# Order of the score products, the weights' transposes and three copies in a windowed-attention stack, and of one copy in a causal attention

## The reference, cut to what matters

```python
mod = (silu(c) @ wmod).reshape(8, 6, 1, 128)         # sa, ca, ga, sb, cb, gb
h = layernorm(x) * (1 + ca) + sa                     # x: 8 x 512 x 128
x = x + ga * attention(h)                            # causal, 16 heads of 8 channels
h = layernorm(x) * (1 + cb) + sb
for i in range(6):                                   # 16 heads of 64 channels
    t = shift_tokens(h)
    q, k, v = split(t @ Wqkv[i])                     # 512 x 1024 each
    q, k = rotary(l2norm(q) * qs, l2norm(k) * ks)
    s = 8 * q @ k.T                                  # windows of 32, each sees itself and the one before
    h = softmax(mask(s)) @ v @ Wo[i] + h
    t = shift_tokens(h); a, g = split(layernorm(t) @ W1[i] + b1[i])
    h = (a * gelu(g)) @ W2[i] + b2[i] + h
x = x + gb * h
```

## Time and profile before

| what | value |
|---|---|
| median of three executions | 4340.35 us |
| the profiled execution, its own time | 4333.15 us |
| its span in the profile | 4331.4 us |
| granted TensorE clock over the span | 0.98 of full speed |
| first attention / stack / last part, about | 0 to 780 / 780 to 4306 / 4306 to 4331 us |

### The profile page before, as it was taken

One profiled execution on the slowest core, in us unless ns is written; L12 is line 12 of the kernel. 1 busy time (PEld: TensorE's weight loads), 2 busy tenths in 40 slices (PEclk: granted clock), 3 DMA queues, 4 the chain that ended last, 5 costly groups with the idle time before them and its releaser, 6 DMA issues. The chain is left out here.

```text
span 4331.4 us, 109584 instructions
## 1 busy us (share of the span) xinstructions
PE 3791.1 (88%) x42284; PEld 2925.6 (68%) x42284; DVE 3346.0 (77%) x4472; ACT 2494.9 (58%) x3301; POOL 2742.1 (63%) x2200
## 2 busy tenths in 40 slices
PE   5888887499998999998999989999899998999996
PEld 3555555377777777777777767777677776777774
DVE  3555555488888888888888878888888888788884
ACT  2555555266665666665666656666566665566663
POOL 2444442276766676766676767676767677767772
PEclk9999999699999999999999999999999999999998
DMA  1111110222223222222222222222322223222221
GB/s 39 46 63 67 68 61 13 65 67 58 56 57 90 66 56 57 59 77 71 62 60 54 66 85 63 55 64 53 87 65 64 56 57 87 64 62 56 57 56 59
DMA packets 157178, 267.01 MB, mean 62 GB/s; under 512 B 32062, under 2 KB 51644, under 8 KB 152380
## 3 DMA queue, kind: packets, MB, share of 16 engines
q1 hardware_dynamic: 157116, 266.19, 22.9%
HBM read 44.81 MB, written 26.21 MB: 16 GB/s over the span
## 5 line engine op out<-in xcount | busy, mean ns | idle before, releaser
L817 POOL TENSOR_TENSOR st_qk_rot<-st_qk_rot,st_qk_sq 128x1024 f32<-128x1024 f32 x384 | 920.6, 2398 | 919.1 <-DVE st_qk_sq L714 919.1
L457 PE MATMUL st_ps<-st_wqkv,st_xs 128*128 128x512 f32 x3456 | 957.8, 413 | 76.2 <-DMA st_wqkv<-wqkv_parts 38.1
L565 ACT ACTIVATE st_qk_sq<-st_ps 128x1024 f32<-128x1024 f32 x384 | 394.0, 1026 | 662.3 <-PE st_ps L457 661.7
L457 PEld LDWEIGHTS st_ps<-st_wqkv,st_xs 128*128 128x128 f32 x3456 | 613.1, 191 | 240.4 <-issue 134.6
L837 POOL TENSOR_TENSOR st_qk_rot<-st_qk_rot,st_rn 128x1024 f32<-128x1024 f32 x384 | 723.1, 1904 | 15.1
L696 DVE TENSOR_REDUCE st_nt<-st_qk_sq 128x16 f32<-128x1024 f32 x384 | 465.6, 1212 | 184.8 <-ACT st_qk_sq L565 184.7
L714 DVE TENSOR_TENSOR st_qk_sq<-st_ps,st_rot 128x512 f32<-128x512 f32 x768 | 490.2, 678 | 0.0
L700 DVE TENSOR_TENSOR st_qk_rot<-st_ps,st_rot 128x1024 f32<-128x1024 f32 x384 | 465.9, 1213 | 7.8 <-PE st_ps L472 7.8
L1444 DVE TENSOR_REDUCE at_nmx<-at_s 128x1 f32<-128x512 f32 (+3 forms) x512 | 238.1, 487 | 296.4 <-PE at_s L1094 295.6
L472 PE MATMUL st_ps<-consts_sb,st_qk_rot 128*128 128x128 f32 x3072 | 402.3, 274 | 27.8 <-DVE st_hid L797 16.7
L465 PEld LDWEIGHTS st_ps<-st_oT,st_wo 128*128 128x128 f32 x3072 | 368.8, 192 | 79.4 <-issue 74.9
(11 more groups left out here) (141 smaller groups left out, 6732.8 us busy)
## 6 DMA issues: line engine op xcount, KB each, us to landing
st_v_bd<-st_v_tok SPq DMA_DIRECT2D x1152, 128.0 KB, 2.4
st_v_bd<-st_v_tok SPq DMA_DIRECT2D x672, 64.0 KB, 2.1
wqkv_parts<-at_w_parts SPq DMA_DIRECT2D x18, 1024.0 KB, 4.6
st_wqkv<-wqkv_parts SPq DMA_DIRECT2D x18, 1024.0 KB, 5.5
at_w_raw<-in_wqkv SPq DMA_DIRECT2D x18, 512.0 KB, 5.2
rotary_tables<-at_rot SPq DMA_DIRECT2D x6, 512.0 KB, 3.3
st_rot<-rotary_tables SPq DMA_DIRECT2D x24, 128.0 KB, 2.4
st_wo<-in_wo SPq DMA_DIRECT2D x6, 512.0 KB, 4.4
```

Of the source, the lines that this page charges most:

```text
L457: last = pe.matmul(out[:, c * 512:(c + 1) * 512], xs[:, x_part, t * P:(t + 1) * P], rhs, start=(n == 0), stop=(n == len(PASSES) - 1))
L565: act.activation(qk_sq[:, cols_of(a)], slot_of("qk"[a], 0, t), ACT.Square).then_inc(squared[a], 1)
L817: pool.tensor_tensor(qk_rot[:, cols], qk_rot[:, cols], qk_sq[:, cols], ALU.add).then_inc(rot_done[a], 1)
```

## The change

In the stack: (1) on PE sim goes ahead of pt; sim takes banks 6 and 7 and pt takes banks 2 and 3, the pair of the other; the single-bank jobs m1, m2 and y move from bank 7 to bank 1 and z from bank 6 to bank 0. (2) On ACT the copy of v goes ahead of the exponential. (3) On ACT the two instructions of the reciprocal norm go ahead of the copy of pt. (4) On DVE the softmax sum and its reciprocal go from behind L772 to right behind the maximum L739, ahead of L745, L749, L756, L764 and L772. In the first attention: (5) on ACT `pick_shifted` goes from the end of the step to right behind the exponential of unit 1, ahead of that of unit 2.

```diff
-            feed = {3: [(("m1", -1, 0), (7,))], 0: [(("m2", -2, 0), (7,))], 1: [], 2: [(("y", -2, 0), (7,))]}[t]
+            feed = {3: [(("m1", -1, 0), (1,))], 0: [(("m2", -2, 0), (1,))], 1: [], 2: [(("y", -2, 0), (1,))]}[t]
             hidden = [(("h", -2, j), H_BANKS[j]) for j in range(HC)] if t == 1 else []
             return [tile("q", 0, 0, 1), tile("tq", 1, 2, 3), tile("k", 0, 4, 5), tile("tk", 1, 6, 7),
-                    tile("v", 0, 2, 3), tile("ot", 3, 0, 1), tile("pt", 2, 6, 7), tile("sim", 1, 2, 3), *feed,
-                    tile("z", 3, 6), tile("o", 2, 4, 5), *hidden]
+                    tile("v", 0, 2, 3), tile("ot", 3, 0, 1), tile("sim", 1, 6, 7), tile("pt", 2, 2, 3), *feed,
+                    tile("z", 3, 0), tile("o", 2, 4, 5), *hidden]
...
@@ scalar, stack
-                        if alive(u, d2):
-                            act.wait_ge(shifted, n - 2)
-                            act.activation(s[:, t2 % 2, :], s[:, t2 % 2, :], ACT.Exp).then_inc(exp_ready, 1)
                         if alive(u, 0):
...
                             act.activation(v_tok[:, par, :], slot_of("v", 0, t), ACT.Copy).then_inc(taken["v"], 1)
+                        if alive(u, d2):
+                            act.wait_ge(shifted, n - 2)
+                            act.activation(s[:, t2 % 2, :], s[:, t2 % 2, :], ACT.Exp).then_inc(exp_ready, 1)
...
+                        if alive(u, 0):
+                            reciprocal_norm()
                         if alive(u, d2):
...
                             act.activation(probT[:, :], slot_of("pt", d2, t2), ACT.Copy).then_inc(taken["pt"], 1)
-                        if alive(u, 0):
-                            reciprocal_norm()
@@ vector, stack
                             dve.tensor_reduce(mx[:, par, :], scores, AX.X, ALU.max).then_inc(max_ready, 1)
+                        if alive(u, d2):
+                            dve.wait_ge(exp_ready, n - 2)
+                            dve.tensor_reduce(den[:, t2 % 2, 0, :], ...).then_inc(den_ready, 1)
+                            dve.wait_ge(den_ready, 2 * (n - 2) - 1)
+                            dve.reciprocal(den[:, t2 % 2, 1, :], den[:, t2 % 2, 0, :]).then_inc(den_ready, 1)
...
                             last.then_inc(taken["z"], 1)
-                        if alive(u, d2):
...
@@ scalar, first attention
                                 if h % GROUP == GROUP - 1 and alive(b, d):
                                     max_parts(b, d, h // GROUP)
+                            if u == 1:
+                                d, h = head_of(s, LAG - 1)
+                                if alive(b, d):
+                                    pick_shifted(b, d, h)
...
-                        d, h = head_of(s, LAG - 1)
-                        if alive(b, d):
-                            pick_shifted(b, d, h)
```

More of the change, by code:

```diff
@@ L739, in unit @@
                             dve.tensor_reduce(mx[:, par, :], scores, AX.X, ALU.max).then_inc(max_ready, 1)
+                        if alive(u, d2):
+                            dve.wait_ge(exp_ready, n - 2)
+                            dve.tensor_reduce(den[:, t2 % 2, 0, :], s[:, t2 % 2, :].rearrange("p (h k) -> p h k", h=HEADS),
+                                              AX.X, ALU.add).then_inc(den_ready, 1)
+                            dve.wait_ge(den_ready, 2 * (n - 2) - 1)
+                            dve.reciprocal(den[:, t2 % 2, 1, :], den[:, t2 % 2, 0, :]).then_inc(den_ready, 1)
                         if t == 3 and alive(u, -1):
```

## The result

The changed kernel took 4167.38 us (median of 4 executions, 4166.82 to 4174.56) against 4340.39 us (4337.48 to 4353.66) of the kernel before on the same chip: a ratio of 0.9599, with a 95% interval of 0.9577 to 0.9622. It is 4% faster; the forecast was 4178 us.

The account below looks back on a forecast made before the run. PE was taken as the bound, waiting for ACT's exponential in the stack and the copy of q in the attention. 4333.15 - 82 (stack) - 80 (attention) = 4171, plus 7.2 for the median: 4178 us; 8-in-10 range 4145 to 4280.

Parts of the forecast that it names:

- attention: First attention: the copy of q falls into ACT's idle time, gaining 80 of PE's 85.3 us wait; bounds 40 and 92.
- tile t = 3: Stack, 15.81 us from q to q: 0.7 us gained, with DVE's chain, not PE, setting the next q.
- tile t = 0: Stack, 15.97 us: DVE's chain ends 15.7 us after q, next q near 15.85; gain 0.1 us.
- tile t = 1: Stack, 20.92 us: L684 is served earlier, h starts near 15.55 us after q against 15.76; gain 0.2 us.
- tile t = 2: Stack, 18.27 us: DVE is done before PE, so the gap and the restart are gained, 0.7 us.
- The gap ahead of pt: Stack: PE's wait for ACT's exponential, 0.59 us in each of 147 tiles, goes when sim runs first.
- my own sign of being wrong: Stack: the prediction fails if PE stands over 0.3 us ahead of q in t = 3 or t = 2.
- Hidden at no cost: Stack: the earlier reciprocal norm and earlier copy of v on ACT delay nothing; cost zero.
- The copy of q brought all, not half: Rival, first attention: norm chains get late behind the moved copy, gain only 40 us, 4218 us; chance 0.10.
- The stack's gap didn't only move: Rival, stack: PE waits for q's banks instead of the exponential in every tile, no gain, 4260 us; chance 0.06.
- L684 didn't stay behind L865: Rival, tile t = 1: L684 stays late, tile costs 1.9 us more, stack 19 us slower, 4279 us; chance 0.06.
- POOL doesn't keep the port: Rival, tile t = 1: POOL's back-to-back instructions block L764, h starts 6.6 us late, 4505 us; chance 0.06.

Follow-up runs that it names:

- the third experiment: The changed kernel with the softmax sum and its reciprocal put back behind the add of z on DVE: 4103.2 us, ratio 0.9442.

## Why the prediction was right

The total came out 11 us under the forecast, 4167 for 4178. The mechanism held, but that the total is so near is in part luck: the stack gave 11 us less than forecast, the attention 15.5 more, and the 7 us added for the distance of the median from the profiled execution were not there in the changed kernel (0.4).

| term | forecast | measured |
|---|---|---|
| tile t = 3 | 0.7 gained (15.1) | 0.50 (15.31) |
| tile t = 0 | 0.1 (15.85) | 0.51 (15.46) |
| tile t = 1 | 0.2 | 0.0 (20.93) |
| tile t = 2 | 0.7 (17.55) | 0.96 (17.31) |
| regular unit | 1.7 (69.3) | 1.96 (69.01) |
| whole stack | 82 us | 71 us |
| attention | 80 us | 95.5 us |

- **The gap ahead of pt** went as said: the wait is gone, the exponential ends ahead of pt's turn, L735 starts 9.93 after q in t = 3 as worked out.
- **t = 3.** DVE's chain ends 14.9 after q, forecast 15.0; but q starts 0.39 behind it, for which I took 0.14. In t = 0 that distance is 0.05. Why it is longer in t = 3 no run shows; the q behind t = 3 is also the first product of a new turn of the loop over units, which was not tried apart. The 0.40 us of PE's idle time ahead of that q also meets my own sign of being wrong (over 0.3). The sign was set too tight, since what I wrote of q, that DVE sets its start, is what happened.
- **t = 0.** L735 starts at 10.50 as said. I added up 0.74 from L749 to the z add and measured 0.54, the sum and its reciprocal took 0.1 less, and the last step 0.05, not 0.14.
- **t = 2.** PE sets this tile, as said. I counted the gap (0.57 in the tile before) and 0.1 for the restart, which no run shows by itself. From sim's start to that of y it is 2.82 (2019.65 to 2022.47) where from pt's it was 3.09 (2071.15 to 2074.24): the order itself is worth 0.27 more.
- **t = 1.** L684 was served at POOL's boundary, ahead of L865, as forecast, and this is the step on which the sign of the result hung. But the second L837 ended 2.36 after q, not 1.9: I took POOL's time from the unit before, while q itself had moved up against it. So L684 ended at 2.91, L735 started at 10.74 instead of 10.4, L771 at 14.56 instead of 14.3, and the 0.2 were lost. I also wrote that the change doesn't touch ot's wait for the first L714 pair. It did, by the same early L684: 1.4 us less in t = 1. PE got to h earlier by that and stood there for the z add, which the softmax sum holds back, so none of it was gained.
- **Hidden at no cost** was wrong for the early norm. I asked who on ACT and POOL needs it and when, and not what POOL's earlier L837 collides with. At the ends of five layers it met L771. With the regular gain of 1.96 x 48 = 94 us against 71 measured, 23 us are missing; there the pair of units took 79.0 + 70.7, where 76.7 + 69.0 are to be had, 4 us each: some 2 for the later h, and at four of the five 1.6 us or more for h at the lower clock, a term that the prediction did not have.
- **The attention.** I took 80 of 85.3 us, "some 96 with the ends of the block", and 95.5 is what came. The waits for L1280 all went, those of the ends too (96.1 us). But the agreement is luck: some 25 us came back as other waits, more than I took off, and PE's busy time, for which my sum has no term, fell by 24.
- **The rivals.** The copy of q brought all, not half. The stack's gap didn't only move. L684 didn't stay behind L865. POOL doesn't keep the port: each L684, L764 or L771 looked at went in at the next end of a POOL instruction, though another was queued, if it had been asked for at least 0.094 us ahead of that end (the last section has those that were not). But the place named for that rival, L764 coming behind L837's start, is the right one. It happens in the changed kernel at five places (2.14 us each) and in the kernel with edit 4 alone in every regular unit (2.19; 1.8 at the ends of layers). Its price at the port is at most one of the two L837 (1.90 us), not 5.67; what it set off on PE, the lower clock, came on top.

The Trainium skill ("SBUF — State Buffer", section "Who interferes with whom") has VectorE and GpSimd share a pair of ports that one instruction holds to its end. The 2.19, 2.14 and 1.43 above, each with one POOL instruction waited out and no second, agree.

What I judged worst was edit 4. I priced it by its effect on the head of the tile (L684 earlier) and found a gain of 0.2 in t = 1; by the third experiment it costs 64 us of the 237 that edits 1, 2, 3 and 5 bring. Pricing each edit against the change without it would have shown this: in t = 1 the sum stands 1.5 us ahead of what h waits for, while L684 ends only 0.4 earlier than with the sum late (2.91 after q, and 1.79 + 1.51 = 3.30 in the third experiment).

## What to carry to other kernels

When the busiest engine waits for one engine's result in each tile, first let it do other ready work, as edit 1 does; that alone may be the whole gain. Work that nobody waits for yet (a sum needed at the tile's end) belongs behind what the busiest engine waits for. When any edit moves DVE against POOL, compare the starting times of the DVE instructions that POOL can hold up with those of POOL's instructions: a margin of half a microsecond can hide a cost of some 3% that comes up as soon as another edit is left out. And when a standstill of the busiest engine grows, look at the granted clock behind it: part of the price may stand there.

## What was not expected of the hardware

A DVE tensor_scalar whose start lay within 0.04 us of that of a POOL tensor_tensor, at 2192.19 even 0.01 ahead of it, lost the whole of that instruction, 2.19 us for 0.48, but never more, in any of the traces. The same holds for L684 at 1.79 with L865 pushed to 2.35, and for L764 at 1.43 between two L817. The POOL instruction next in line is what gets longer: the first L837 kept its 1.90 us, the second took 2.08, and so the two take 3.94 there and 3.76 elsewhere.

To go in at the next end, the DVE instruction must be there a little before it. In the kernel before L684 meets the end of POOL's second L837 in most units; these rows stand around the two L684 of the earlier trace rows:

```profile
2039.59 3.77 POOL L837 TENSOR_TENSOR st_qk_rot<-st_qk_rot,st_rn 128x1024 f32<-128x1024 f32 x2
...
3190.03 3.77 POOL L837 TENSOR_TENSOR st_qk_rot<-st_qk_rot,st_rn 128x1024 f32<-128x1024 f32 x2
...
3193.75 2.46 POOL L865 TENSOR_TENSOR st_s<-st_s,st_mx 128x1024 f32<-128x1024 f32 x1
```

The first L684 was asked for 0.07 us ahead of the end of L837 and stood for all of L865, 2.48 us in all; the second was asked for 0.094 ahead, took its 0.74, and L865 was stretched. Over all 14 traces each of the 78 L684 that came 0.058 to 0.089 us ahead of such an end (36 of them in the kernel before) waited for the POOL instruction behind it too, and no L684, L764 or L771 did that came 0.094 or more ahead. So 36 units of the kernel before lost 1.7 us at L684 by some hundredths of a microsecond. Edit 4 brings L684 0.4 us forward in that kernel and out of it: there it took 1.0 us.

A standstill of PE of 2.54 us ahead of h was followed by a granted clock of 0.76 over h in 29 of 46 units of the kernel with edit 4 alone, and h took 7.1 us for 5.4. At the standstills of 1.66 us there in the regular units of the changed kernel h always took 5.4.
